# Transposing the high and low part of the keys as one set in the second layer of a two-layer transformer kernel

## What is computed

```python
q5 = (x @ Wq).reshape(b, t, H, E, DH)            # H = 8 heads, E = 5 experts, DH = 64
k5, v5 = split((x @ Wkv).reshape(b, t, 2, H, E, DH))
q = einsum('bthed,bthe->bhtd', q5, sd_g)         # sum over experts, weighted by gates
k = einsum('bthed,bthe->bhtd', k5, ss_g)
v = einsum('bthed,bthe->bhtd', v5, ss_g)
attn = softmax(einsum('bhid,bhjd->bhij', q * scale, k))
out = einsum('bhij,bhjd->bihd', attn, v)         # then a projection by expert
```

## Time and profile before

| | |
|---|---|
| median of three runs (lowest, highest) | 1698.67 us (1687.71, 1700.9) |
| the profiled execution, its own time | 1687.58 us |
| its span, first to last instruction | 1685.8 us |
| mean granted TensorE clock, share of full speed | 0.966 |
| TensorE matmul (PE) | 1556.2 us busy, 92% |
| TensorE weight load (PEld) | 1012.7 us, 60% |
| VectorE (DVE) | 1254.2 us, 74% |
| ScalarE (ACT) | 939.7 us, 56% |
| GpSimd (POOL) | 847.9 us, 50% |

### The profile page before, as it was taken

How to read it: one execution, slowest core, us unless ns; L and a number is a source line. 1 busy time by engine, 2 the same in 40 slices (tenths; PEclk the granted TensorE clock), 3 DMA queues, 4 the chain that set the end, 5 groups by cost and what they waited for, 6 DMA issues and landing times.

```text
span 1685.8 us, 27140 instructions
## 1 busy us (share of the span) xinstructions
PE 1556.2 (92%) x8404; PEld 1012.7 (60%) x8404; DVE 1254.2 (74%) x2518; ACT 939.7 (56%) x1582; POOL 847.9 (50%) x935
## 2 busy tenths in 40 slices
PE   4699999999999976689999999999999999999998
PEld 2455565565565545466666666567576666666555
DVE  3997787687679536777887778787778787777664
ACT  3446756756755631344655655655655656556652
POOL 2530000000001133458869879788689699698452
PEclk9599999999999987989999999999999999999998
DMA  2000000000000000000000000000000000000000
GB/s 64 0 1 1 2 1 2 1 1 1 1 1 1 1 12 13 1 1 13 0 13 1 1 13 2 0 13 1 13 1 1 13 1 1 1 1 1 1 7 19
DMA packets 12230, 9.39 MB, mean 6 GB/s; under 512 B 3840, under 2 KB 11584, under 8 KB 12096
## 3 DMA queue, kind: packets, MB, share of 16 engines
q1 hardware_dynamic: 12096, 7.66, 1.7%
HBM read 6.61 MB, written 1.05 MB: 5 GB/s over the span
## 4 chain that ended last, share of the span: by engine, by line
PE 63%; POOL 18%; DVE 9%; issue 4%; ACT 4%; SPq 1%; DMA 0%; DVEq 0%; ACTq 0%; POOLq 0%
PE ps L887 10%; PE ps L700 9%; PE ps L734 7%; PE ps L719 7%; PE ps L860 5%; PE ps L875 5%; POOL gs L1526 4%; PE ps L667 4%; PE ps L876 4%; POOL gsum L1527 3%; POOL z L572 3%; POOL onm L566 3%; PE ps L898 2%; POOL h_qk L1528 2%; DVE mxp L1201 2%
## 5 line engine op out<-in xcount | busy, mean ns | idle before, releaser
L1080 ACT ACTIVATE pbuf<-ps 128x512 f32<-128x512 f32 x512 | 301.6, 599 | 170.4 <-PE ps L876 166.2
L976 ACT ACTIVATE pbuf<-ps 128x1024 f32<-128x1024 f32 (+3 forms) x320 | 280.1, 897 | 182.5 <-PE ps L722 92.2
L1201 DVE TENSOR_REDUCE mxp<-ps 128x1 f32<-128x512 f32 (+2 forms) x432 | 279.1, 685 | 82.8 <-PE ps L700 51.4
L1407 DVE TENSOR_TENSOR den<-den,pbuf 128x1024 f32<-128x1024 f32 x224 | 312.8, 1396 | 1.9
L887 PE MATMUL ps<-pbuf,h_v 128*64 128x512 f32 x1024 | 248.7, 606 | 0.0
L1066 ACT ACTIVATE relu<-ps 128x512 f32<-128x512 f32 x256 | 152.2, 599 | 161.2 <-PE ps L860 132.1
L1359 DVE TENSOR_TENSOR gt<-ps,gate 128x320 f32<-128x320 f32 x384 | 181.6, 483 | 78.4 <-POOL h_v L1536 36.4
L700 PE MATMUL ps<-kM,qT 128*128 128x512 f32 (+3 forms) x640 | 230.9, 414 | 9.2 <-ACT kM L963 4.9
L875 PE MATMUL ps<-q1T,k1T 128*128 128x512 f32 x512 | 215.3, 421 | 11.4 <-ACT pbuf L1080 9.9
L1380 DVE CUSTOM_DVE_ANT_0 relu<-ps,relu 128x512 f32<-128x512 f32 x256 | 174.2, 684 | 64.5 <-PE ps L860 61.7
L719 PE MATMUL ps<-qT,kM 128*128 128x512 f32 (+3 forms) x640 | 199.5, 381 | 8.5 <-ACT pbuf L976 8.5
(11 more groups left out here) (224 smaller groups left out, 2799.5 us busy)
## 6 DMA issues: line engine op xcount, KB each, us to landing
wraw<-in_Wkv SPq DMA_DIRECT2D x16, 160.0 KB, 2.5
wraw<-in_Wq SPq DMA_DIRECT2D x8, 160.0 KB, 2.3
out<-x SPq DMA_DIRECT2D x4, 256.0 KB, 2.3
wqkv<-in_wqkvT SPq DMA_DIRECT2D x1, 192.0 KB, 3.9
masks<-in_masks SPq DMA_DIRECT2D x1, 128.0 KB, 4.1
dft<-in_dft SPq DMA_DIRECT2D x1, 128.0 KB, 2.3
wout<-in_Wo SPq DMA_DIRECT2D x2, 64.0 KB, 2.6
ident<-in_ident SPq DMA_DIRECT2D x1, 64.0 KB, 5.8
```

The costliest lines, as they stand in the source:

```text
L976: nc.scalar.activation(pbuf0[:, u % NP0, :, off:CH], ps[:, b:b + 2, off:CH], ACT.Exp, scale=float(D0) ** -0.5).then_inc(s_exp, 1)
L1080: nc.scalar.activation(pbuf1[:, u % NP1, i, :], ps[:, i, :], ACT.Exp, scale=float(D1) ** -0.5).then_inc(s_exp1, 1)
L1201: v.tensor_reduce(mxp[:, i, h:h + n, b], sc.rearrange("p (h k) -> p h k", h=n), AX.X, ALU.max).then_inc(s_read0d, 1)
L1407: v.tensor_tensor(dn, dn, w, ALU.add).then_inc(s_den1, 1)
```

## The change

The low part of the keys goes into the second half of `sk1`, `sk2` disappears, and the keys of a chunk take one set of four transposes: high part in rows 0 to 63 of the bank, low part in rows 64 to 127. ScalarE copies the high rows twice, once to rows 0 to 63 and once across to rows 64 to 127 of `k1T`, and the low rows from 64 to 127 down to rows 0 to 63 of `k2T`. `hik` writes 256 elements of each partition where it wrote 512. So a chunk has two `t` steps where it had three; they stand at 3.7 and 4.1 units. The rest of the diff follows from the new numbering.

```diff
-    t = [[("t", 0, c, w) for w in range(3)] for c in range(NC)]
+    t = [[("t", 0, c, w) for w in range(2)] for c in range(NC)]
...
-                out += [(end + STAGE1[2] + 0.3 * w, ("t", h, c, w)) for w in range(3)]
+                out += [(end + STAGE1[2] + 0.4 * w, ("t", h, c, w)) for w in range(2)]
...
-                    pe.wait_ge(s_stq if w == 2 else s_stk, NC * h + c + 1)
-                    src = (sk1, sk2, sq1)[w]
-                    chunk_transposes(ring1, step, lambda i: src[:, i, :], D1 if w == 1 else P).then_inc(s_turn1, 1)
+                    pe.wait_ge(s_stq if w else s_stk, NC * h + c + 1)
+                    src = (sk1, sq1)[w]
+                    chunk_transposes(ring1, step, lambda i: src[:, i, :]).then_inc(s_turn1, 1)
...
-                        wait_turn(act, ring1, ("t", h, c - 1, 1) if c else ("t", h - 1, NC - 1, 1))
-                    nc.scalar.activation(sk1[:].rearrange("p n (a d) -> p n a d", a=2).bitcast(F32R),
-                                         h_qk[:, 1, TPC * c:TPC * (c + 1), :].unsqueeze(2).to_broadcast([P, TPC, 2, D1]),
+                        wait_turn(act, ring1, ("t", h, c - 1, 0) if c else ("t", h - 1, NC - 1, 0))
+                    nc.scalar.activation(sk1[:, :, 0:D1].bitcast(F32R), h_qk[:, 1, TPC * c:TPC * (c + 1), :],
                                          ACT.Copy).then_inc(s_hik, 1)
...
+                    if w == 0:
+                        nc.scalar.activation(k1T[h % 2][0:D1, q], ps[0:D1, b, :], ACT.Copy)
+                        nc.scalar.activation(k1T[h % 2][D1:P, q], ps[0:D1, b, :], ACT.Copy)
+                        nc.scalar.activation(k2T[h % 2][0:D1, q], ps[D1:P, b, :], ACT.Copy).then_inc(s_read1a, 1)
+                    else:
+                        nc.scalar.activation(q2T[h % 2][0:D1, q], ps[0:D1, b, :], ACT.Copy)
+                        nc.scalar.activation(q1T[h % 2][:, q], ps[:, b, :], ACT.Copy).then_inc(s_read1a, 1)
...
-                    v.tensor_tensor(sk2[:, :, 0:D1], h_qk[:, 1, TPC * c:TPC * (c + 1), :], sk1[:, :, 0:D1],
+                    v.tensor_tensor(sk1[:, :, D1:P], h_qk[:, 1, TPC * c:TPC * (c + 1), :], sk1[:, :, 0:D1],
                                     ALU.subtract).then_inc(s_stk, 1)
```

More of the change, by code:

```diff
@@ L99, in first_head @@
     out = [("gates",)] + k[0:4]
[L100 to L103, removed]
+    out += [q[0], q[1], hik[0], q[2], q[3], lok[0], k[4], k[5], hiq[0], k[6], t[0][0], k[7], loq[0]]
+    out += [k[8], hik[1], k[9], k[10], t[0][1], lok[1], k[11], k[12], hik[2], k[13], t[1][0]]
+    out += [k[14], lok[2], k[15], kd[0], v[0], t[2][0], hik[3], v[1], dif[0], dif[1], mx[0], lok[3]]
+    out += [dif[2], mx[1], v[2], t[3][0], kd[1], dif[3], mx[2], v[3], mx[3]]
     out += [dif[4], dif[5], mx[4], dif[6], mx[5], dif[7], mx[6], mx[7], ("m", 0, 0), ("q2", 0, 0)]
@@ L112, in first_head @@
         end = at(TPC * c + TPC - 1) + 0.2
-        out += [(end + 1.2, hiq[c]), (end + 1.8, loq[c]), (end + 2.6, t[c][2])]
+        out += [(end + 1.2, hiq[c]), (end + 1.8, loq[c]), (end + 2.6, t[c][1])]
     return out
@@ L319, in build @@
         sk1 = s1("sk1", [P, TPC, P])
-        sk2 = s1("sk2", [P, TPC, D1])
         sq1 = s1("sq1", [P, TPC, P])
@@ L852, in _ @@
                     bank = take(ring1, step)
-                    wait_read(pe, ring1, ("t", h, it // TPC, 2))
+                    wait_read(pe, ring1, ("t", h, it // TPC, 1))
                     wait_read(pe, ring1, ("t", h, 2 * p + 1, 0))
@@ L1047, in _ @@
                     if h or c:
-                        wait_turn(act, ring1, ("t", h, c - 1, 2) if c else ("t", h - 1, NC - 1, 2))
+                        wait_turn(act, ring1, ("t", h, c - 1, 1) if c else ("t", h - 1, NC - 1, 1))
                     nc.scalar.activation(sq1[:, :, 0:D1].bitcast(F32R), h_qk[:, 0, TPC * c:TPC * (c + 1), :],
@@ L1055, in _ @@
                         act.wait_ge(s_sc1, 2 * U1 * (h - 1))
[L1056 to L1060, removed]
+                    q, b = slice(CH * c, CH * (c + 1)), ring1.bank(step)
+                    if w == 0:
[5 more added lines that the diff above has]
+                        nc.scalar.activation(q1T[h % 2][:, q], ps[:, b, :], ACT.Copy).then_inc(s_read1a, 1)
                 elif kind == "dif":
```

## The result

The kernel with the change took 1704.16 us, the kernel before 1696.08 us, each the median of 20 runs. The ratio as measured, which is not the quotient of the two medians (1.0048), is 1.0055, with a 95% interval of 1.004 to 1.007: 9.3 us slower (6.8 to 11.9). 7.7 us faster was forecast. A second series of the same kernel gave 1.0052 (1.0027 to 1.0077). The profiled execution took 1706.46 us.

A forecast was written before the change was run, and what follows sets the result against it. The prediction took TensorE and GpSimd to bound the kernel in turns. Its terms, -9.2 + 1.3 + 0.2 = -7.7 us, took the median of 1698.67 to 1691.0 us (chance 0.60), with an 8-in-10 range of 1673 to 1709 us.

The forecast's parts named there:

- Transposes: TensorE, seven heads: a set less saves 0.44 us in chunks 0, 2 and 3, nothing in chunk 1; 9.2 us off.
- the whole record goes: Rival: each transpose saved is worth its whole record of 0.272 us, 22.8 us in place of 9.2; 1677.4 us; chance 0.07.
- 0.18 us stays: Chunk 2, ScalarE: 0.92 us asked of a cover of 0.74, so 0.18 us stays; 1.3 us back over seven heads.
- I take nothing there: Chunk 3: the exponential comes 0.48 us later, but a V pair stands before the score steps that wait; no cost.
- called "nothing": Chunk 0: the exponential comes 0.96 us later against 2.3 us of slack before the second score step; no cost.
- So 0.48 us more: ScalarE, each chunk: a third copy of the keys adds 0.48 us, the distance from one copy's start to the next.
- The crossing costs double: Rival: two crossing copies cost 0.59 us more in 14 chunks (2 and 3); +8.8 us, 1707.5 us; chance 0.06.
- First head: +0.2 us: First head: no set saved helps, kd is just in time behind three copies; +0.2 us, at worst +1.9.
- the block of three copies delays the exponential: Rival: TensorE loses 0.96 us and gains 0.44 in each of 28 chunks; +14.6 us, 1713.3 us; chance 0.10.
- the forecast's 30 and the rival's 45: Sign: line 875's weight load waits near 30 us for exponentials if the forecast holds, near 45 if the slower rival does.
- A head period still at 118 us, with GpSimd's share of the chain over 32%: Sign over the later heads that would prove TensorE wasn't what set the pace; the forecast itself had 116.9 us.
- Within 1%: Whole kernel: the time stays within 1% of before, neither below 1681.7 nor above 1715.7 us; chance 0.81.

The follow-up runs named there:

- two_in_place: Changed kernel with the keys' set copied out twice, both copies on the partitions they read, no crossing (operands not the reference's); 1689.78 us, 0.9946 to 0.9993 of before.
- three_in_place: two_in_place plus a third copy of 64 rows, in place, into a spare tile; no crossing; 1698.60 us, 0.9988 to 1.004 of before.
- before_halves: Kernel before with the copy to k1T cut into two halves, each on its own partitions; 1699.22 us, 0.9997 to 1.004 of before.
- first_only: Kernel before with the single set of transposes and three copies in head 0 alone; 1697.71 us, 0.9993 to 1.0024 of before.

## Why the prediction was wrong

- **Transposes: right in the chunks that pay, and nearly in the sum.** 0.44 us for each set in three chunks of four is 1.32 us a head; two_in_place measured 1.47, with the shorter `hik` in it: 0.38, 0, 0.75 and 0.37 us in chunks 0 to 3. The record of 272 ns was rightly not the price, and "the whole record goes" is refuted: three chunks at 1.09 us would be 3.3 us a head. Chunk 1 kept GpSimd in the chain.
- **"0.18 us stays" and "I take nothing there": the step that failed.** The forecast let the additional copy be covered but for 0.18 us in chunk 2; that is 0.18 us a head, and three_in_place measured 1.57. What it had wrong is the cover: the copy stands in the same line as the transposes (set, copies, exponential, score matmul), and it pushes an exponential that had stood between the copies behind all of them.

Chunk 3 was put at nothing and costs 0.92. The exponential that counts stood between `k1T` and `k2T`, and the score matmul that waits for it began 1.00 us after its end, ahead of the `V` pair and not behind it. These two rows of before were missing beside the earlier trace rows:

```profile
952.92 0.59 ACT L1080 ACTIVATE pbuf<-ps 128x512 f32<-128x512 f32 x1
954.51 0.40 PE L875 MATMUL ps<-q1T,k1T 128*128 128x512 f32 x1
```

That exponential began 0.50 us behind the first copy. Behind three copies it begins 1.45 us behind the first one in place and 1.82 with the crossing, a push of 0.95 or 1.32 us, while TensorE arrives 0.44 us sooner: 1.39 or 1.76 us against 1.00. The row above has the score matmul idle for 0.66. (In three_in_place a second wait helps make the 0.92: there the transposes stand 0.36 us for VectorE's low part in every one of these heads, in two_in_place in none.) In before_halves the push is 1.22 - 0.50 = 0.72 us and TensorE comes no sooner, and that is covered.

Chunk 2 was put at 0.18 and costs 0.48. The idle time before `k2T` and `q2T` was counted as cover, but it lay around an exponential that stood between the keys' copies and the queries', missing beside the earlier trace rows:

```profile
940.70 0.58 ACT L1080 ACTIVATE pbuf<-ps 128x512 f32<-128x512 f32 x1
```

After, ScalarE goes through all five copies first, and the next exponential starts 2.78 us after the first of them (1194.08 to 1196.86) instead of 1.32; the score matmul behind it stands idle for 0.81.

Chunk 0 was called "nothing" for its 2.3 us of slack and costs 0.17 for the copy, 0.48 with the crossing. The slack was that of the score step, but a relu follows the exponential and comes later too, and a projection waits for that relu, by 0.28 us in each of the five heads. After:

```profile
1036.54 0.41 PE L841 MATMUL ps<-wh,xh 128*128 128x320 f32 x1 [0.28 <-ACT relu L1067]
```

- **"So 0.48 us more": mis-sized.** It was read between `k2T` and `q2T`, which both start at partition 0. With changed starts the group takes 1.82 us. The prediction priced the crossing by the length of its record, 588 ns, which was right (590 and 595 measured), and never asked for the distance to the next start. Against three_in_place this is +0.52 to +0.75 us a head. "The crossing costs double" had the right place and the wrong form.
- **"First head: +0.2 us", at worst 1.9: too small.** At like clock the stretch grew by about 3 to 4.5 us. That no saved set helps there was right. By the times first_only lost only 1.4 us (at most 4.1). The third copy is not most of it (two_in_place, 184.7 us); what else makes it, turns of the banks, `kd` or the order, stays open.
- **The rival "the block of three copies delays the exponential"** was the right mechanism: its sign was to be the score matmul's waits, and they grew, by 8.3 us on the weight loads over five heads; over 810 us (756 to 1566) they are 39.5 us where before had 30.1, between the forecast's 30 and the rival's 45. Its size was not right: it had +0.52 us in each of 28 chunks, 2.1 us a head, where 0.62 to 0.85 came. In chunk 1 neither gain nor loss shows.
- **A sign that would have misled.** "A head period still at 118 us, with GpSimd's share of the chain over 32%" was to prove that TensorE didn't set the pace. Both came (118.65 us, and 33.2% over the five heads), yet two_in_place shows that TensorE's transposes were worth 1.47 us a head.
- **The sum.** A head: -1.47 + 1.57 + 0.52 = +0.62 us, where the forecast had -1.07 (its own terms, -9.2 + 1.3 over seven heads, give -1.13). Seven heads at 0.62 to 0.85 give +4.3 to +6.0 us; with 3 to 4.5 us in the first head that is 7.3 to 10.5, and 9.3 was measured. The agreement is better than its parts: by the times alone the later heads are +0.5 us (at most 3.4) and the first +1.4, and nothing that was tried accounts for the rest. "Within 1%" held, the direction didn't; the range of 1673 to 1709 us held the time, mostly because it was set by rivals and by the scatter of the first three runs.

## What to carry to other kernels

Before a copy is traded for matmuls, look at which line both stand in: where the copy and the transposes follow each other on the way to the next exponential, 0.44 us off TensorE and 0.48 us onto ScalarE can be a loss. List every instruction that the new block pushes back, the exponential and what follows it, and compare the push, plus what TensorE gains, with the slack of each step that waits. A longer ScalarE alone tells nothing: 0.86 us more a chunk cost 0.11 us a head in before_halves. Price an instruction by the distance to the next start, and take that distance from a pair that changes partitions as the new pair will. Compare stretches between steps that both kernels share before two spans are subtracted: here half of 18.9 us lay ahead of the change.

## What the runs showed of the hardware that I had not expected

- ScalarE overlapped consecutive instructions of 512 elements from PSUM by 0.09 to 0.11 us (0.48 to 0.50 start to start, 0.59 the record) where both started at the same partition; where one started at 0 and the other at 64, the distance was 0.58 to 0.62 between copies and to the exponential behind.
- A crossing between the partition halves costs ScalarE nothing of its own: 590 and 595 ns against 587 in place, by the groups of the changed kernel:

```profile
L1058 ACT ACTIVATE k2T<-ps 64x512 fp32r<-64x512 f32 x32 | 19.0, 595 | 0.4
L1057 ACT ACTIVATE k1T<-ps 64x512 fp32r<-64x512 f32 x32 | 18.9, 590 | 0.4
L1056 ACT ACTIVATE k1T<-ps 64x512 fp32r<-64x512 f32 x32 | 18.8, 587 | 13.9 <-PE ps L666 13.7
```

- The granted clock between 650 and 690 us was anything from 0.50 to 0.80 in executions of kernels that are alike up to there, which moved the last `gate` copy between 676 and 688 us.
